# A pre-norm transformer layer: how the first batch is set up before the attention stream starts

## The reference, cut to what matters

```python
def attn(x):                                  # x is normalised already
    q, k, v = split(x @ in_proj_weight.T + in_proj_bias)      # 16 heads, HD = 16
    scores = (q / sqrt(16)) @ k.T
    scores = where((j <= i) & (j >= i - 16), -inf, scores)
    return (softmax(scores) @ v) @ out_proj_weight.T + out_proj_bias

def ffn(x):
    return tanh(((x @ weight) @ aux_weight1) @ aux_weight2 + bias)

x = x + attn(layernorm(x))
x = x + ffn(layernorm(x))
```

## Time and profile before

| | us |
|---|---|
| median of 3 runs | 2262.78 |
| lowest, highest | 2254.99, 2266.57 |
| the profiled execution, its own time | 2252.17 |
| the span in its profile | 2250.2 |
| PE busy in the span | 1903.2 (85%) |
| ACT busy in the span | 1986.7 (88%) |
| DVE, POOL busy in the span | 614.5 (27%), 182.8 (8%) |

### The profile page before, as it was taken

The page is one execution under the profiler, slowest core; times in us unless marked ns, Lnnn a source line. Parts: engine busy times, 40 slices in busy tenths (PEclk is TensorE's granted clock), DMA queues, the critical chain, the costliest instruction groups (busy, mean ns, idle before and its releaser), DMA issues. The chain is left out here.

```text
span 2250.2 us, 76375 instructions
## 1 busy us (share of the span) xinstructions
PE 1903.2 (85%) x34896; PEld 678.5 (30%) x34896; DVE 614.5 (27%) x1208; ACT 1986.7 (88%) x2106; POOL 182.8 (8%) x173
## 2 busy tenths in 40 slices
PE   2749899998889999898988989898998888888882
PEld 1412233332323333233332323333332222222221
DVE  6602132322223232322322223232321111111112
ACT  1349999999899999999988999999999999999980
POOL 5200010001001000100100000010100000000000
PEclk8869999999999999999999999999999999999995
DMA  2251010102331010201134021110033010101000
GB/s 80 86 75 33 24 43 21 53 24 57 57 56 48 21 53 24 57 29 41 44 47 75 24 57 29 40 46 29 26 52 72 14 43 14 42 16 34 17 23 25
DMA packets 85996, 92.80 MB, mean 41 GB/s; under 512 B 19104, under 2 KB 73888, under 8 KB 85664
## 3 DMA queue, kind: packets, MB, share of 16 engines
q1 hardware_dynamic: 85664, 87.81, 16.5%
HBM read 53.09 MB, written 26.28 MB: 35 GB/s over the span
## 5 line engine op out<-in xcount | busy, mean ns | idle before, releaser
L1099 ACT ACTIVATE probs<-scores 128x1024 f32<-128x1024 f32 x2048 | 1948.0, 1057 | 126.4 <-PE scores L1121 88.8
L1140 PE MATMUL outs<-probs,vs 64*32 64x512 f32 x16384 | 1079.2, 592 | 8.4 <-issue 8.3
L1121 PE MATMUL scores<-qs,ks 49*32 49x512 f16 x16384 | 838.1, 383 | 243.4 <-ACT probs L1099 181.7
L1121 PEld LDWEIGHTS scores<-qs,ks 49*32 49x32 f16 x16384 | 233.3, 89 | 1257.3 <-ACT probs L1099 1095.0
L1140 PEld LDWEIGHTS outs<-probs,vs 64*32 64x32 f32 x16384 | 290.6, 106 | 75.5 <-issue 32.2
L830 DVE TENSOR_TENSOR probs<-probs,allowed 128x320 f32<-128x320 f32 (+2 forms) x280 | 138.6, 495 | 352.6 <-ACT probs L1099 352.5
L1162 PE MATMUL spare<-s_xt,w_qkv 128*128 128x512 f32 x192 | 108.0, 645 | 0.0
L779 POOL TENSOR_TENSOR s_squares<-s_qk_f 128x512 bf16<-128x512 f32 x48 | 61.3, 1278 | 460.9 <-DVE s_qk_f L890 460.9
L1204 PE MATMUL spare<-w_o,ctx_in 128*128 128x256 f32 x256 | 74.0, 415 | 22.7 <-DVE ctx_in L855 22.7
L773 POOL TENSOR_TENSOR s_x<-s_x,bias_o 128x1024 f32<-128x1024 f32 x16 | 38.0, 2374 | 480.1 <-DMA s_x<-in_x 480.1
L890 DVE TENSOR_SCALAR s_qk_f<-spare,bias_qk 128x512 f32<-128x512 f32 x48 | 36.0, 750 | 149.9 <-PE spare L1162 149.9
(11 more groups left out here) (97 smaller groups left out, 671.5 us busy)
## 6 DMA issues: line engine op xcount, KB each, us to landing
qs<-q_parts SPq DMA_DIRECT2D x192, 64.0 KB
ks<-k_parts SPq DMA_DIRECT2D x48, 256.0 KB
ctx_in<-raw SPq DMA_DIRECT2D x256, 32.0 KB, 2.0
s_x<-in_x SPq DMA_DIRECT2D x16, 512.0 KB, 4.1
inverse<-row_inverse SPq DMA_DIRECT2D x256, 32.0 KB, 1.9
out<-s_pre SPq DMA_DIRECT2D x16, 512.0 KB, 2.9
s_xin<-in_x SPq DMA_DIRECT2D x12, 512.0 KB, 3.9
q_parts<-s_parts SPq DMA_DIRECT2D x24, 256.0 KB, 2.1
```

What stands on the lines that cost most here:

```text
L1099: act.activation(probs[:, u % RING, 2 * slot:2 * slot + 2].rearrange("p c q -> p (c q)"), scores[:, 2 * slot:2 * slot + 2].rearrange("p c ...
L1121: last = pe.matmul(scores[cols, 2 * slot + e], ks[rows, group, keys], qs[rows, group], start=True, stop=True)
L1140: last = pe.matmul(outs[32 * c:32 * c + 32, side], vs[keys, at:at + 2 * HD], probs[keys, u % RING, c], start=(i == 0), stop=(i == KBLOCKS ...
```

## The change

- **GpSimd's fills.** `vs[0]` and `vs[1]` are no longer filled as a whole; only the columns of ones and the 32 elements at the end are set. The four fills of `ks` are gone. A small tile `guard_row` (8 rows of 2048) is filled once and goes through the DRAM tensor `guard_keys` into rows 48 and 112 of `ks`. The head mask is made after `rsqrt(0)` in place of before it.
- **SP's order.** The weights are issued second. `bias_v` has a semaphore of its own. The loads of `w_o`, `bias_o` and `bias_f` come last, behind the guards, and SP waits for them at the end of the block. Batch 0's keys load chunk by chunk: 12 loads of 64 KB for each of the four chunks, each set behind the stores of the chunk after it. The 12 query loads go with chunk 0's keys.
- **Guards** go from the SBUF tile `guard` straight to the rows of `qs`, in the prologue and in the stream.
- **The ffn fold** moves to step 0 of the stream: three loads at its start, four matmuls each at r = 22 and r = 50, one DVE copy each at r = 24 and r = 53.
- **Sums of squares** come between the two halves of the values on PE, and their reduction between the two halves on DVE.
- **The inverse** is loaded by two DMAs of 256 KB a step in place of 16 of 32 KB.

```diff
-def load_keys(sp, lay, b, hg, k_parts):
+def load_keys(sp, lay, b, hg, k_parts, tokens):
...
-            sp.dma_start(lay["ks"][rows, hg * QUADS:(hg + 1) * QUADS], src).then_inc(lay["qs_in"][hg], 16)
+            src = k_parts[b * HALVES + hg, FAST_K[r], :, tokens].rearrange("(u e d) t -> e d u t", e=2, d=HD)[e]
+            sp.dma_start(lay["ks"][rows, hg * QUADS:(hg + 1) * QUADS, tokens], src).then_inc(lay["qs_in"][hg], 16)
...
-def load_guards(sp, lay, b, hg, guards):
+def load_guards(sp, lay, hg, guard):
...
+        sp.dma_start(lay["qs"][row:row + 1, hg * QUADS:(hg + 1) * QUADS],
+                     guard[hg * PASS_HEADS + e:(hg + 1) * PASS_HEADS:2]).then_inc(lay["qs_in"][hg], 16)
...
             sp.dma_start(xin[:, 0], x_tiles[0]).then_inc(x_in[0], 16)
-            for dst, src in ((a1t, a1_t), (a2s, a2), (w1t, w1_t)):
-                sp.dma_start(dst[:], src.rearrange("(h p) n -> p h n", p=P)).then_inc(ffn_in, 16)
+            sp.dma_start(w_qkv[:], w_qkv_t.rearrange("(h p) n -> p h n", p=P)).then_inc(w_qkv_in, 16)
...
+            sp.wait_ge(cleared, 1)
+            sp.dma_start(guard_keys[0], guard_row[:]).then_inc(guard_row_out, 16)
+            sp.wait_ge(guard_row_out, 16)
+            for e in range(2):
+                row = e * HALF_P + FAST_DOT
+                sp.dma_start(lay["ks"][row:row + 1], guard_keys).then_inc(rest_in, 16)
+
+            def load_chunk(cc):
+                sp.wait_ge(parts_out[cc % 2], (cc // 2 + 1) * 64)
+                for hg in range(HALVES):
+                    if cc == 0:
+                        load_queries(sp, lay, 0, hg, q_parts)
+                    load_keys(sp, lay, 0, hg, k_parts, slice(cc * CHUNK, (cc + 1) * CHUNK))
...
-            for par in range(2):
-                sp.wait_ge(parts_out[par], CPB // 2 * 64)
-            for hg in range(HALVES):
-                load_queries(sp, lay, 0, hg, q_parts)
-                load_keys(sp, lay, 0, hg, k_parts)
-            sp.wait_ge(guard_done, 1)
-            sp.dma_start(guards[0], guard[:]).then_inc(guard_out, 16)
-            sp.wait_ge(guard_out, 16)
-            for hg in range(HALVES):
-                load_guards(sp, lay, 0, hg, guards)
+                if cc:
+                    load_chunk(cc - 1)
+            load_chunk(CPB - 1)
+            sp.wait_ge(guard_done, 1)
+            for hg in range(HALVES):
+                load_guards(sp, lay, hg, guard)
+            sp.dma_start(keep["w_o"][:], w_o_t.rearrange("(h p) n -> p h n", p=P)).then_inc(rest_in, 16)
+            for dst, src in ((keep["bias_o"], b_o), (keep["bias_f"], b_f)):
+                sp.dma_start(dst[:], src.partition_broadcast(P)).then_inc(rest_in, 16)
             sp.wait_ge(rest_in, 5 * 16)
...
+            def set_ones(buffer, count):
+                columns = lay["vs"][buffer][:, 0:KBLOCKS * V_ROW].rearrange("p (n d) -> p n d", d=V_COLS)
+                pool.memset(columns[:, :, HD:V_COLS], 1.0).then_inc(cleared, 1)
+                pool.memset(lay["vs"][buffer][:, KBLOCKS * V_ROW:], 1.0).then_inc(cleared, 1)
+                pool.wait_ge(cleared, count + 2)
+
+            rsqrt(0)
+            pool.wait_ge(consts, 4)
+            pool.wait_ge(rstd_done, 1)
+            pool.memset(guard_row[:], GUARD_K).then_inc(cleared, 1)
...
+            set_ones(0, 1)
+            rsqrt(1)
...
-            for hg in range(HALVES):
-                for e in range(2):
-                    pool.memset(lay["ks"][e * HALF_P + 32:(e + 1) * HALF_P, hg * QUADS:(hg + 1) * QUADS],
-                                GUARD_K).then_inc(cleared, 1)
...
             rsqrt(3)
-            pool.memset(lay["vs"][1][:], 1.0).then_inc(cleared, 1)
+            set_ones(1, 5)
...
-            pe.wait_ge(ffn_in, 3 * 16)
-            for stage, (left, right) in enumerate(((a1t, a2s), (w1t, a12))):
...
             pe.wait_ge(w_qkv_in, 16)
-            pe.wait_ge(a12_copied, 2 * HALVES)
...
                 for kb in range(KPC):
+                    if kb == KPC // 2:
+                        sum_squares(c)
...
                 for hg in range(HALVES):
-                    for h in range(PASS_HEADS):
-                        head = hg * PASS_HEADS + h
-                        sp.dma_start(inverse[h * HD:(h + 1) * HD, hg],
-                                     row_inverse[head].partition_broadcast(HD)).then_inc(inverse_in, 16)
+                    heads = row_inverse[hg * PASS_HEADS:(hg + 1) * PASS_HEADS]
+                    sp.dma_start(inverse[:, hg], heads.unsqueeze(1).to_broadcast([PASS_HEADS, HD, CHUNK])
+                                 ).then_inc(inverse_in, 16)
...
+            def fold_ffn(stage):
+                if stage == 0:
+                    pe.wait_ge(ffn_in, 3 * 16)
+                    pe.wait_ge(qk_copied, 1)
+                else:
+                    pe.wait_ge(a12_copied, 1)
+                    pe.wait_ge(v_copied, 1)
+                left, right, done = ((a1t, a2s, a12_ready), (w1t, a12, ffn_ready))[stage]
+                for half in range(HALVES):
+                    for k in range(HALVES):
+                        last = pe.matmul(spare[stage][:, half * EMB:(half + 1) * EMB],
+                                         left[:, k, half * P:(half + 1) * P], right[:, k],
+                                         start=(k == 0), stop=(k == HALVES - 1))
+                last.then_inc(done, 1)
...
+                    if step == 0 and r in (22, 50):
+                        fold_ffn((r - 22) // 28)
```

More of the change, by code:

```diff
@@ L244, in _ @@
                 sp.dma_start(keep["bias_v"][side * HALF_P:(side + 1) * HALF_P],
[L245 to L248, removed]
+                             b_v_sides[side].partition_broadcast(HALF_P)).then_inc(bias_v_in, 16)
+            sp.wait_ge(cleared, 1)
[10 more added lines that the diff above has]
+                    load_keys(sp, lay, 0, hg, k_parts, slice(cc * CHUNK, (cc + 1) * CHUNK))
             for cc in range(CPB):
@@ L442, in _, with sum_squares @@
             turn(0, 1)
-            pe.wait_ge(ffn_in, 3 * 16)
-            for stage, (left, right) in enumerate(((a1t, a2s), (w1t, a12))):
-                if stage:
-                    pe.wait_ge(a12_copied, HALVES)
-                for half in range(HALVES):
-                    for k in range(HALVES):
-                        last = pe.matmul(ps_w[:, 2 * stage + half], left[:, k, half * P:(half + 1) * P], right[:, k],
-                                         start=(k == 0), stop=(k == HALVES - 1))
-                    last.then_inc(a12_ready, 1)
-            pe.wait_ge(w_qkv_in, 16)
-            pe.wait_ge(a12_copied, 2 * HALVES)
+            pe.wait_ge(w_qkv_in, 16)
+            def sum_squares(c):
+                pe.wait_ge(squared, c * 4 + 4)
+                if c < CPB - 1:
+                    pe.wait_ge(turn_copied, c * 2 + 4)
+                if c == 0:
+                    pe.wait_ge(consts, 7)
+                for j in range(4):
+                    at = 32 * (j // 2)
+                    last = pe.matmul(ps_norm[at:at + HEADS], head_of[:, j % 2], squares[:, j],
+                                     start=(j % 2 == 0), stop=(j % 2 == 1))
+                last.then_inc(norms_ready, 1)
             def step(c):
@@ L484, in step @@
                         last.then_inc(v_ready, 1)
-                pe.wait_ge(squared, c * 4 + 4)
-                if more:
-                    pe.wait_ge(turn_copied, c * 2 + 4)
-                for j in range(4):
-                    at = 32 * (j // 2)
-                    last = pe.matmul(ps_norm[at:at + HEADS], head_of[:, j % 2], squares[:, j],
-                                     start=(j % 2 == 0), stop=(j % 2 == 1))
-                last.then_inc(norms_ready, 1)
             for c in range(CPB):
@@ L510, in masked_columns, with stream @@
     return (lo, hi - lo, lo - at) if lo < hi else None
-def stream(nc, keep, lay, x, q_parts, k_parts, guards, row_sums, row_inverse, out):
+def stream(nc, keep, lay, x, w1_t, a1_t, a2, q_parts, k_parts, row_sums, row_inverse, out):
     with ExitStack() as ctx:
@@ L557, in stream @@
         shift = sb("s_shift", [HEADS, 1])
-        guard = sb("s_guard", [HEADS, CHUNK], F16)
+        guard = lay["guard"]
         fine = sb("s_fine", [P, 1])
@@ L721, in run_step @@
                     if qc == 0:
-                        load_keys(sp, lay, b, 1, k_parts)
-                        load_guards(sp, lay, b, 1, guards)
+                        load_keys(sp, lay, b, 1, k_parts, slice(0, SEQ))
+                        load_guards(sp, lay, 1, guard)
                     start_chunk(step - 1)
@@ L1012, in run_step @@
                         split_low(step, 1)
+                    if step == 0 and r == 24:
+                        dve.wait_ge(a12_ready, 1)
+                        dve.tensor_copy(a12, spare[0][:].rearrange("p (h n) -> p h n", n=EMB)).then_inc(a12_copied, 1)
+                    if step == 0 and r == 53:
+                        dve.wait_ge(ffn_ready, 1)
```

(2 more changed lines are left out.)

110 lines of the change are left out of this document (50 added, 60 removed).

## The result

The kernel after takes 2206.69 us (median of 4, 2205.87 to 2207.36), the kernel before 2260.49 us (median of 4, 2254.99 to 2266.57) in the same measurement. The ratio is 0.9761, with an interval of 0.9734 to 0.9788: 53.8 us less by the medians. The forecast was 58.8 us less, 2204 us. The profiled execution after took 2206.76 us with a span of 2202.9, so profile against profile the gain is 45.4 us of time and 47.3 of span; why these two differ from 53.8 and from 58.8 is a part of what follows.

The account below looks back on a forecast made before the run. Prediction: the stream keeps ACT and PE busy, so the gain lies in prologue holes; 36.9 + 20.0 + 4.3 - 2.4 = 58.8 us off 2262.8 gives 2204 us, range 2186 to 2224, chance 0.77.

Parts of the forecast that it names:

- The bound: Whole kernel: ACT and PE busy 88% and 85%, mostly unchanged stream work, so gains were sought where neither works.
- the two holes: Prologue: only DMA works between about 110 and 137 us; chunk 1's normalising takes 27.56 us beside GpSimd's fills of ks.
- The compute of the prologue: Prologue up to chunk 3's last part: gains of 7.4, 26.6 and 2.9, sum 36.9 us, last part at 66.1.
- SP behind the compute: From last part to first score: 19.0 us in place of 39.0, gain 20.0, bounds 15 and 22.
- Transfers of 64 KB: Batch 0's key loads: transfers keep up with issue at 0.46 us each, taking 200 GB/s; at 125, 2 us later.
- The fold: Step 0: two groups of matmuls cost ACT 1.2 us each, 2.4 in all, bounds 0.7 and 4.
- The inverse: Behind the last step: two 256 KB loads take 3.5 to 5.5 us, not 8.8; gain 4.3, bounds 3 and 5.5.
- The guards' shorter way in the stream brings nothing.: Stream: no gain found, as PE's gap while the next batch's keys load is ended by issue, not a guard.
- The engines starved of instructions: Rival, prologue: loads beside the compute cost each chunk a 3.8 us PE gap, 15 us, time 2219; chance 0.08.
- the 10.6 us: Whole kernel: the runs' median lies 10.6 us above the profiled execution, so the forecast became 2204, not 2193.4.

Follow-up runs that it names:

- the slices: The kernel after, with the stream's keys of batches 1 to 3 also loaded in four slices of 64 KB loads: 2190.36 us.
- run 277: Not a run's label: 277 is the count of instruction packets over the whole run of the kernel before, one in 8.1 us.
- two queues: Sliced stream keys, context moved first, earlier w_o and biases, last chunk's keys also from ACT's queue, fold in four, PE busy early: 2158.41 us, 0.9562 of the kernel before.

## Why the prediction was right, point by point

- **The bound.** Right: the gain lay before the first score, and the two holes named were the ones that closed.
- **The compute of the prologue**, 36.9 us forecast, 102.96 - 66.91 = 36.1 measured: 8.2 for 7.4 in chunk 0, 24.8 for 26.6 from chunk 0 to 1, which is just below the bound of 25, and 3.2 for 2.9 from chunk 2 to 3. The fills alone, tried by themselves, moved the last part from 102.96 to 70.40, 32.6 us. Chunk 0's start came at 19.39 in place of the 20.2 forecast: GpSimd began 0.7 us earlier, and its small fills took less from DVE than I gave them. Two things ate this. One was not in the sum: the slow first matmuls of the projection, 1.7 us, since the fold that I took off the path had also kept PE running in front of it. The other is the period of 12.27 us in place of 12.12. One reading was wrong, without weight in the sum: that a normalising group ends about 1.4 us behind the fill holds for chunk 0 (19.51 against 18.12) and nearly for chunk 3 (1.3), not for chunk 1, where 58.93 is only 0.15 behind 58.78. Its 27.56 us are four instructions of about 7 us, one to each of the four fills; under a single fill the three that are left run behind it.
- **SP behind the compute**, 19.0 us forecast, 87.11 - 66.91 = 20.2 measured. 24 loads took 12.47 us, 0.52 each on the average in place of 0.46, which is the 1.4 that was missing. The landing of the last bias took 2.7 us from the end of its issue, where I had 2.5. The rest is right to a few tenths. Loading the keys whole again took 18.1 us back, near the 18.8 that this term had gained (39.0 - 20.2).
- **Transfers of 64 KB.** The choice of 200 GB/s over 125 was right in that the transfers kept up: the loads ran at share 0.49 and 138 GB/s, the rate at which SP issued them, and nothing here shows what one queue could have reached. The Trainium skill's rule in "DMA: Bandwidth & Descriptors", section Bandwidth, that transfers want to be 1 MiB or more, would by its 0.95 us for one of 64 KB have made the sum 23 us smaller, an estimate. Its figures are for transfers to 128 partitions issued from GpSimd, where these go to 16 partitions and are issued by SP. Here the measurement decides against it: the last 24 loads were issued in 12.47 us and the first score came 7.3 us behind them, and the loads of 256 KB ran full at 123 GB/s. No run here has loads of 1 MiB.
- **The fold**, 2.4 us forecast, 2.6 measured. Right, with its reason: 1.4 and 1.2 us for the 1.2 each of the forecast, and 1.5 us in four pieces of the length for which 0.38 was read.
- **The inverse**, 4.3 us forecast, 3.8 measured. The landing took 3.6 us behind the last issue, inside the 2.1 to 4.2 forecast; the two issues took 1.32 us in place of 0.9, which is most of what is missing. From 2160 to 2162 us the DMA share is 0.49 to 0.53 at 188 to 201 GB/s, though nothing else is running. The Trainium skill, "DMA: Bandwidth & Descriptors", section on why a DMA increments its semaphore by 16, says that a transfer is spread over the largest number of engines, up to 16, that divides the slowest dimension of both sides; here these are 8 heads and 128 partitions, so 8 of 16, which the trace agrees with. The share alone doesn't prove it, as the key loads that waited for SP's issue ran at 0.49 too.
- **"The guards' shorter way in the stream brings nothing."** Right as far as the traces show: the gaps stand at the same places after. It wasn't tried by itself.
- **The engines starved of instructions** was a rival for the prologue, priced at 15 us with chance 0.08. There it didn't come, the DMA engines being at half load. But I read the row for it only as a price. It was the largest loss left in the stream, and it differed by 8.5 us between the two profiled executions. So the forecast against the profiled execution, 2193.4, missed by 13.4 us: 8.5 from these gaps, 2.7 from the measured terms (56.1 against 58.8), 1.9 from the time around the span (3.9 us after, 2.0 before), and 0.3 that I can't place. Against the median it missed by 2.7. That it came so near is in part luck: the 10.6 us that I added to come from the profile to the runs made up for most of the 13.4, and they rested on three runs and one profiled execution of the kernel before.

## What to carry to other kernels

A fill on GpSimd is not free because GpSimd is idle: beside the fills here DVE's normalising from SBUF to SBUF stood for their whole length, so fill only what will be read, and let a DMA bring constants. Follow the row on which a wait ends at "issue" to what the DMA engines did at that time; spreading the loads and ordering SP's queue by who needs what first won another 33 us on top of the change. When a loss varies from run to run, a forecast made against one profiled execution carries that luck.

## What was not expected of the hardware

- **While long loads fill the DMA engines, PE comes to a stand.** Key loads of 4 KB rows keep the DMA engines at share 1.0 to 1.1, and some 11 to 12 us after the first of them PE stands, for up to 6.3 us at a time and for nothing but "issue", in all seven profiled kernels that load the stream's keys whole (26 to 40 us of ACT's gaps in a run). With 1 KB rows at share 0.5 none of these gaps is left; the slices changed the length of the rows and the share together, so that the runs don't tell them apart. The kernel before shows something in its list of queues too: no instruction packet completed between 600 and 612 us, two between 612 and 620, where over the whole run 277 of them come to one in 8.1 us.

```profile
q1 hardware_dynamic: 501, 1.50, 91.9%
```
```profile
q1 hardware_dynamic: 579, 0.56, 47.0%
q8 instruction: 2, 0.03, 2.2%
```

  (The stretches are 600 to 612 and 612 to 620 us; packets, MB, share.) That PE's instructions queue behind the data is the reading that the experiments support; it is not shown, as the list of queues doesn't say which engine a packet was for.
- **Rows of 4 KB load slower than rows of 1 KB** into the same 16 partitions: mostly 119 to 131 GB/s in stretches of 2 us against 161 to 200 with full engines, of which 161 to 189 were with two queues. Why stays open.
- **At the start of the kernel PE runs slowly, and the clock column doesn't show it.** The column reads 1.00 (2.4 GHz) from the start, though PE has done nothing. In the kernel after, weight loads of chunk 0's projection took 0.34 us until 22.5 and 0.19 from then on, as at the lower and the higher of the two levels, while the granted clock of both stretches is given as 1.00:

```profile
22.09 0.34 PEld L473 LDWEIGHTS ps_qk<-xt,w_qkv 128*128 128x128 f32 x1 [0.52 <-issue]
22.88 0.19 PEld L473 LDWEIGHTS ps_qk<-xt,w_qkv 128*128 128x128 f32 x1 [0.46 <-issue]
```
```profile
20.00:22.00 2.00, 2.00 (x3) 0.68 (x2) 0.00 (x0) 0.00 (x0) 0.30 (x1) 1.00 0.00 0
22.00:24.00 2.00, 2.00 (x5) 0.91 (x4) 0.20 (x1) 0.92 (x2) 0.00 (x0) 1.00 0.00 0
```

  The turn in front of it took 1.94 us there and 1.04 in the later chunks. Behind later rests the column does show it: in the kernel before PE had stood for 24 us, and chunk 1's turn at 58.98 took 1.97 us at a granted clock of 0.50 (1.2 GHz). With PE busy before it, none of the group's weight loads took longer than 0.19.
